# A deformable convolution's gathers wait for ScalarE's copies of the turned taps, not for TensorE's turns

## The reference

```python
off_out = conv(x, w_off) + b_off                  # 27 maps: 9 dy, 9 dx, 9 masks
py = gy + ky + dy                                 # [B, 9, H, W], one place for each of 9 taps
px = gx + kx + dx
mask = sigmoid(mask)
v00, v01, v10, v11 = x at the four corners around (py, px), zero outside
sampled = (v00*(1-wy)*(1-wx) + v01*(1-wy)*wx
           + v10*wy*(1-wx) + v11*wy*wx) * mask    # [B, C, 9, H, W]
out = einsum('oik,bikhw->bohw', weight.reshape(Co, C, 9), sampled)
out = relu(out * scale + (beta - run_mean * scale))
```

## Time and profile before

| | |
|---|---|
| median of 3 runs | 11114.93 us (11110.37 to 11115.27) |
| profiled execution, span from first to last instruction | 11102.5 us |
| median less that span | 12.4 us |
| stage b in the profiled execution | from 4296 to 5345 us, 1049 us (9.4% of the span) |
| gathers in stage b | 648 (72 tiles of 9), first at 4344.5, last at 5302.3 us |
| granted TensorE clock, whole span | 0.939 |
| granted TensorE clock, stage b | 0.71 to 0.83 in stretches of about 250 us |

### The profile page before, as it was taken

How to read it: one execution, slowest core, us unless ns; L and a number is a source line. 1 busy time by engine, 2 the same in 40 slices (tenths; PEclk the granted TensorE clock), 3 DMA queues, 4 the chain that set the end, 5 groups by cost and what they waited for, 6 DMA issues and landing times. The chain is left out here.

```text
span 11102.5 us, 159680 instructions
## 1 busy us (share of the span) xinstructions
PE 9398.8 (85%) x56794; PEld 4972.7 (45%) x56794; DVE 7584.7 (68%) x8585; ACT 6067.6 (55%) x12476; POOL 5542.6 (50%) x3721
## 2 busy tenths in 40 slices
PE   7888888888888775776899899999899998799897
PEld 3333333343333333666555555555555554433334
DVE  5999999999999995666666555555555553344633
ACT  4666666667666663111466666656666665233233
POOL 5888888989888885666333232222223320011010
PEclk8999999999999998887999999989999998899988
DMA  2222222222222223666100000000000001200003
GB/s 71 75 79 77 79 78 79 77 79 82 76 81 78 78 78 112 195 201 188 59 1 4 1 4 1 4 1 4 4 1 4 1 10 41 93 1 1 1 1 140
DMA packets 259082, 623.27 MB, mean 56 GB/s; under 512 B 26280, under 2 KB 114448, under 8 KB 255993
## 3 DMA queue, kind: packets, MB, share of 16 engines
q1 hardware_dynamic: 203672, 438.27, 11.9%
q0 software_dynamic: 51840, 169.91, 5.1%
q10 hardware_dynamic: 2784, 4.87, 0.1%
HBM read 572.05 MB, written 40.90 MB: 55 GB/s over the span
## 5 line engine op out<-in xcount | busy, mean ns | idle before, releaser
L978 POOL TENSOR_TENSOR a_dBu<-a_du,a_Bs 128x960 f32<-128x960 f32 (+1 forms) x1280 | 2716.1, 2145 | 221.2 <-DVE a_H L750 201.1
L750 DVE TENSOR_TENSOR_SCAN a_H<-a_pA,a_dBu 128x962 f32<-128x962 f32 (+1 forms) x1280 | 2655.7, 2075 | 109.6 <-ACT a_pA L919 56.0
L919 ACT ACTIVATE a_pA<-a_delta,a_al 128x480 f32<-128x480 f32 (+1 forms) x2560 | 1624.8, 639 | 1148.7 <-DVE a_H L750 1144.1
L541 PE MATMUL a_pY<-a_H,cst 128*128 128x480 f32 (+1 forms) x5120 | 2212.3, 554 | 34.5 <-ACT a_Y L936 34.2
L758 DVE TENSOR_TENSOR a_H<-a_H,a_pC 128x960 f32<-128x960 f32 (+1 forms) x1280 | 1397.0, 1091 | 84.9 <-PE a_pC L541 83.7
L541 PEld LDWEIGHTS a_pY<-a_H,cst 128*128 128x128 f32 x5120 | 975.3, 193 | 706.0 <-issue 539.5
L541 PE MATMUL a_pC<-a_stk,a_sel 96*128 96x480 bf16 (+1 forms) x1280 | 471.2, 368 | 514.3 <-DVE a_H L758 506.1
L3380 POOL TENSOR_TENSOR e_P<-e_P 128x1024 f32<-128x1024 f32 (+1 forms) x80 | 151.8, 1919 | 1464.8 <-ACT e_P L3356 1464.8
L2441 POOL TENSOR_TENSOR c_KF<-c_KF,c_dg 128x1056 f32<-128x1056 f32 x192 | 385.4, 2007 | 872.7 <-DVE c_MX L2206 872.1
L1089 POOL DMA_INDIRECT b_gath<-b_tab,b_idx x648 | 615.4, 950 | 395.4 <-issue 176.6
L2279 DVE SCALAR_TENSOR_TENSOR X<-c_P,c_be,X 128x384 f32<-128x384 f32 x192 | 118.2, 616 | 919.8 <-PE c_P L1902 919.8
(11 more groups left out here) (463 smaller groups left out, 18332.6 us busy)
## 6 DMA issues: line engine op xcount, KB each, us to landing
a_Bs<-a_brows SPq DMA_DIRECT2D x512, 480.0 KB
a_Bs<-a_brows SPq DMA_DIRECT2D x128, 384.0 KB
d_W<-in_d_w SPq DMA_DIRECT2D x32, 1024.0 KB, 7.7
f_W<-in_f_w SPq DMA_DIRECT2D x32, 1024.0 KB, 7.7
b_tab<-b_TT SPq DMA_DIRECT2D x32, 576.0 KB
b_gath<-b_tab,b_idx POOLq DMA_INDIRECT x648
a_zt<-a_sz SPq DMA_DIRECT2D x36, 256.0 KB
a_sz<-a_zt SPq DMA_DIRECT2D x16, 480.0 KB
```

The source lines that it names most:

```text
L541: return pe.matmul(out, lhsT, rhs, start=start, stop=stop, skip_group_check=True)
L750: v.tensor_tensor_scan(span(H[:, g % NH, :], g), factors(g), span(dBu[:, g % ND, :], g), 0.0, ALU.mult, ALU.add).then_inc(S(kind), 1)
L919: s.activation(pA[:, k, at:at + z], delta[:, u % 2, h, 0:z], ACT.Exp, scale=al[:, o + 2 * d, h, n:n + 1]).then_inc(S(kind), 1)
L978: g.tensor_tensor(inner(dBu[:, i % ND, :], i), du[:, u % 2, :, 0:z], Bs[:, p % NB, i % 2, 0:z].unsqueeze(1).broadcast_to([128, 2, z]), ALU ...
```

## The change

The wait of the gathers counts the semaphore `turn_out`, which ScalarE's copy of a turn raises, in place of `turned`, which the last matmul of the turn raises. Counts and places stay: three of each for each tile, in the same order. Nothing else differs.

```diff
                     for t in range(9):
                         if n >= NG and t % 4 == 0:
-                            g.wait_ge(S("turned"), 3 * (n - NG) + t // 4 + 1)
+                            g.wait_ge(S("turn_out"), 3 * (n - NG) + t // 4 + 1)
                         g.indirect_dma_start(
```

## The result

The changed kernel takes **11141.58 us** (median of 8 runs, 11132.98 to 11146.13) against 11112.12 us (8 runs, 11099.84 to 11116.58) for the kernel before on the same chip: ratio 1.0027, 95% interval 1.0019 to 1.0036. That is 29.5 us slower. The profiled execution has a span of 11131.8 us, 29.3 us more than the earlier trace rows.

A forecast was written before the change was run, and what follows sets the result against it. Stage b was taken as bound by a loop of gather burst and TensorE's next signal; 52 x 0.60 = 31.2 us on the 11102.5 us span gives 11133.7, plus 12.4 to the runs' median 11146 us, range 11111 to 11158.

The forecast's parts named there:

- The loop: Stage b: next signal comes 12.93 us after a gather burst starts, so 0.60 us delay makes period 13.77 us; chance 0.66.
- The size: Stage b: 52 releases each pay 0.60 us, together 31.2 us.
- put at 0: Stage b: the other 16 GpSimd waits, straight behind TensorE's work, were taken to cost 0, at most 9.6 us.
- The waits before taps 4 and 8: GpSimd's later waits in a stage b tile: covered by 4 us or more, so they cost nothing.
- Nobody waits for the rows: Stage b: VectorE has three tiles of gathered rows in hand, so later gathers cost it nothing directly.
- The rest of the program: All later stages start behind a barrier and move as a whole; their lengths stay the same.
- Nothing happens: Rival: TensorE's own chain takes 13.2 us and the burst only happens to land with it; 11115 us, chance 0.22.
- The sum of 0: Stage b: if gathers don't cause TensorE's late signals, the burst moves freely and nothing is added; 11115 us.
- faster: Rival: first turns signal in mid-burst and half of 52 tiles lose their pause, 49 us; 11066 us, chance 0.06.
- turns slip through: Sign that the prediction is wrong: several bursts in a row without a pause before tap 0, with pauses at tap 4.
- Dearer: Rival: all 68 felt waits pay 0.60 us and TensorE's clock drops for a further turn, 62 us; 11177 us, chance 0.06.

The follow-up runs named there:

- plain loads of more bytes: Kernel before with only taps 0, 3 and 6 gathered, plus six plain 262 KB loads a tile on SyncE's queue: 10849.35 us, ratio 0.9765.
- half rows: Kernel before with all nine gathers fetching only the upper corners, 1 KB of each row instead of 2 KB: 11115.06 us, ratio 1.0016.
- 64 partitions: Kernel before with each of nine gathers fetching 64 rows of 2 KB into partitions 0 to 63 instead of 128: 11137.46 us, ratio 1.0025.
- the kernel that waits for the third copy: Kernel before with all three gather waits of a tile counting the third copy (turn_out of tap 8) of tile n-5: 11172.42 us, ratio 1.0061.
- landing: Kernel before, with GpSimd also waiting before tap 0 until the last three gathers of the tile before have landed: 11162.75 us, ratio 1.0064.
- three-gather kernel: Kernel before with only taps 0, 3 and 6 of nine gathered and the gather buffer zeroed once: 10813.76 us, ratio 0.9747.

## Why the prediction was right, and where its reason wasn't

**The loop (the step that carried the sum): right in effect, wrong in its cause.** The copy starts 12.94 us after the burst, as forecast, and 0.60 us more before the burst is 0.6 us more a period. But the prediction put it as "the signal comes when the burst of gathers has landed". The runs say otherwise: half the bytes and half the rows moved the landing from 13.4 to 12.5 and 12.0 us and left the signal where it was, and plain loads of more bytes held little. What the runs leave standing is GpSimd's string of issues, and its length. From the end of its last issue to the copy it is 4879.24 - 4877.28 = 1.96 us before, 4755.63 - 4753.64 = 1.99 after, 1.9 with half rows (4721.37 - 0.24 - 4719.24), 2.24 behind eleven issues, and 2.4 with 64 partitions, where the last issue ends 10.6 us after the start. So it isn't a fixed time behind the last issue either: with thirteen issues it is 5215.71 - (5212.14 + 0.95) = 2.62 us. What fits all of them is a time from the string's start in proportion to the number of issues: 12.9 us for nine (also with half rows and 64 partitions), 15.74 for eleven, 5215.71 - 5197.15 = 18.56 for thirteen, each 1.43 us an issue, while GpSimd itself needs 1.25. Any of these causes gives the same sum for this change, since all are measured from the burst's start. That is why the size came out; for the cause that the prediction named it was luck.

The prediction also said too much with "TensorE's signals don't come before its burst has landed". In nearly every tile one does: the signal of the convolution. In the earlier trace rows ScalarE follows it at 4872.76, 6.45 us into the string. Between the first string, which is longer, and the last gather there are 66 of these signals. In the kernel that waits for the third copy all 66 reach ScalarE in the middle of a string, within 0.04 us of the modelled end of the last record:

```profile
5129.60 0.94 POOL L1089 DMA_INDIRECT b_gath<-b_tab,b_idx  x1 [2.87 <-ACT b_smp L1291]
5133.63 0.46 ACT L1300 ACTIVATE X<-b_pO,b_bn 128x128 f32<-128x128 f32 x1 [4.30 <-PE b_pO L1152]
```

In the kernel before, 62 of the 66 come inside a string, 33 within 0.3 us of that end and the latest 4.7 us behind it. Of the turns, one copy came 6.98 us into a burst (third copy), one 5.63 us (landing), and one 10.01 us into the string of eleven. Signals that are late and still come inside a string keep to a grid: in the kernel before, 67 of the 69 signals of turns, convolutions and `rows` transposes that came over 0.3 us behind their record, and 3 to 12.5 us into a string, lie within 0.12 us of a multiple of 0.717 us from its start, half of 1.43. By chance it would be a third of them.

What stays open is why a string of indirect issues delays the turns' signals, why the convolution's mostly pass, and whether it is the signal or the matmuls' own end that is late: the trace has only the starts of TensorE's records, and their ends are modelled. The bytes and the number of rows don't matter by these runs; what in an issue does, no run shows.

**The size.** 52 x 0.60 = 31.2 us was forecast, 29.3 us of span measured. The price of a steady period was right, 13.80 against 13.77. How many periods pay it was not. Of the periods that start with tiles 8 to 70, the 49 that ended in a "remote" wait before grew by 0.40 us on average, from 13.22 to 13.62, and not by 0.60; the 13 that ended in a wait on TensorE, put at 0, grew by 0.46, from 13.93 to 14.39. So 49 x 0.40 + 13 x 0.46 = 25.6 us, where the working has 49 x 0.60 = 29.4: the two deviations nearly cancel, which is luck.

**The waits before taps 4 and 8: right.** Alone they give 1.0001 [0.9992, 1.0010], and the wait before tap 0 alone gives the full 1.0027.

**Nobody waits for the rows: right.** VectorE's waits on gathers are 6 and 15.0 us in both traces, and a ring of four costs nothing.

**The rest of the program: right within 3 us** (1.3 shorter ahead of the gathers, 2.7 longer behind the stage).

**The rivals.** "Nothing happens" is excluded by the interval. The sum of 0 had the Trainium skill's page "SBUF — State Buffer", section "SBUF: two separate sides", beside it. Its sentence, that a DMA and a compute instruction don't slow each other, isn't contradicted: the transfers turned out not to be the cause, and the three-gather kernel with the plain loads agrees with it in most tiles (267 GB/s, TensorE mostly not held). What was wrong was to conclude from it that the burst could move freely. Of "faster", the signals in mid-burst came, and bunched up: from tile 57 on every second first turn slips through, and the pause moves to tap 4, the sign that the prediction had named for "turns slip through". It saved hardly anything, since the held signal then comes 18.56 us after the start of thirteen issues instead of 12.9 after nine: 13.7 us a tile against 13.8. "Dearer" didn't come: the granted clock in the windows 4500 to 4700 and 4700 to 4900 is 0.80 and 0.79, against 0.82 and 0.80 before, and from 5100 to 5300 it is 0.78 against 0.76.

## What to carry to other kernels

When GpSimd issues indirect DMAs in long strings, read what it waits for before the next string, and by how much the signal trails TensorE's last record: an issue engine that is three tiles ahead of its reader can still be in a loop with the engine that frees its buffers, and then each added 0.6 us in that loop is paid once a tile. To test such a loop, delay one wait at a time and cut the rows that lie ready; if the ring's depth doesn't matter and the delay of the first wait does, it is a loop and not a shortage. The gain to be had lies in fewer issues, not in fewer bytes: in this kernel three instead of nine took 282 us off (with six taps left out), half the bytes took none.

## What the runs showed of the hardware that was not expected

- An indirect DMA of 128 rows costs GpSimd 0.95 us and 0.30 us until the next, with 2 KB or 1 KB rows (950 and 948 ns); with 64 rows still 0.91 us. The price is nearly all per issue.
- The turns' signals mostly reach ScalarE only 1.9 to 2.6 us after GpSimd's string of nine to thirteen issues ends, 1.43 us an issue from its start, though the records of the matmuls end up to 7 us earlier. The convolution's signals mostly come in the middle of the string. With three issues a tile the delay is gone. In the changed kernel's first tiles, where 54 issues follow each other without a pause, ScalarE waits 28.9 us once.
- DMA traffic of 254 to 267 GB/s, more than twice that of the three-gather kernel without the loads (118 and 109 GB/s in the same windows), moved that kernel's ratio from 0.9747 [0.9731, 0.9764] to 0.9765 [0.9749, 0.9781]: the intervals overlap.
